# One SBUF input per blend operation, and a convolution in two passes, in a deformable-convolution kernel

## The chip, the cores and the metric

The kernel runs on one core of a Trainium2 chip. The metric is the time on the device of one execution, in microseconds (us). The engines are named as in the profile: PE (TensorE: matmul and transpose), DVE (VectorE), ACT (ScalarE), POOL (GpSimd) and SP (SyncE), each with its own queue of instructions, held in order by semaphores. SBUF is the on-chip memory, PSUM the eight banks (2 KB per partition each) in which PE leaves its results.

## What is computed

An image `x` of 2 x 128 channels x 64 x 64 goes through a layer norm over channels, then through a block of four deformable convolutions with 1, 1, 9 and 49 taps (60 in all) and 256 outputs each, then group norms, a 1 x 1 fuse and a spectral (FFT) stage. The change lies in the deformable convolutions alone. For each of the 60 taps and each pixel the reference takes four neighbouring pixels ("corners") at a position that is itself computed by convolutions, weighs them, adds them and multiplies the sum with the tap's weights:

```python
offset = conv2d(x, off_w, off_b, pad)
mask = 2.0 * jax.nn.sigmoid(conv2d(x, mod_w, mod_b, pad))
...
v00, v01 = gather(y0, x0), gather(y0, x0 + 1)
v10, v11 = gather(y0 + 1, x0), gather(y0 + 1, x0 + 1)
sampled = (v00 * (1 - wy) * (1 - wx) + v01 * (1 - wy) * wx + v10 * wy * (1 - wx) + v11 * wy * wx) * mask
y = einsum('bckhw,ock->bohw', sampled, reg_w)
```

All of it is in float32.

## The kernel before

`stage_branches` does this work. Its 2 x 4096 pixels are cut into 16 groups (`NG`) of 512 pixels, and the 60 taps of a group follow one another, so there are 960 steps `n` (`NT`), step n being tap `k` of group `g`. Each engine has a loop over n, written out by hand. For a step:

- POOL issues four indirect DMAs (`gather`, L472), one for each 128 pixels. Each takes 128 row numbers from the SBUF tile `om` and brings 128 rows of 2 KB, a row holding the four corners of a pixel, 128 channels each. They land in `G[k % 6]`, one of six buffers (`RING`); POOL waits until the step six before has been blended (`blended`, L486).
- ACT scales the first corner in place with four activations (`corner0`, L507).
- DVE (`blend`) multiplies corners 1 to 3 by their weights, read with stride 0 from the SBUF tile `omw` (L623, 1536 elements per partition); adds corners 2 and 3 to corners 0 and 1 (L629, 1024 elements); and adds the two sums into one of three `acc` buffers (L633, 512 elements). The sum is what frees `G`. Each of the three reads two inputs from SBUF.
- PE turns `acc` (four transposes into one of two PSUM banks `ps_t`, L742); ACT copies that to `sT` (`copy_out`, L515) two steps after the blend of the same tap; PE contracts `sT` with the tap's weights `R` into `ps_y` (`contract`, L754), two steps (`LAG`) behind the turn.

Beside it PE computes the offsets and masks of the next group: 49 taps of a 7 x 7 convolution with 180 output columns, 128 of them into `ps_c` (L724) and 52 into `ps_c2` (L725), spread by `share_at` over 52 of 56 steps (36 steps for the first). `copy_conv` takes the two banks to SBUF, `turn_conv` turns them into the bank `ps_o` in four tiles of 128 pixels, and DVE makes row numbers and weights of each tile (`rows` and `weights`, L585 to L613), sixteen instructions in two neighbouring steps. At tap 54 of a group DVE also takes statistics of finished outputs (`measure`, L639). The eight PSUM banks are all in use: `ps_y` two, `ps_t` two, `ps_c`, `ps_c2`, `ps_o` and `ps_side` (normalisation of the second image) one each.

## Time and profile before

| | |
|---|---|
| time, median of 3 runs | 7700.79 us (7696.2 to 7709.71) |
| the profiled execution | 7701.75 us, its span 7700.1 us |
| granted TensorE clock, mean | 0.886 of 2.4 GHz |
| first to last blend of `stage_branches` | 167 to 6229 us of the span |

The span is the time from the first to the last instruction. The profile gives, for each engine, the time in which it was busy, groups of instructions by line with the mean length of one, and what ended the idle time before them; the trace gives single instructions in order of time. A DMA's row on POOL is the time in which POOL prepares it, not the transfer.

### The profile page before, as it was taken

To read this page: it belongs to the slowest core of one execution; us is meant where nothing else is said; L and a number is where in the kernel's file an instruction comes from. 1 tells how busy PE (TensorE), PEld (TensorE's weight loads), DVE (VectorE), ACT (ScalarE), POOL (GpSimd) and SP (SyncE) were. 2 spreads that over 40 slices of the span, in tenths; PEclk is the share of its full clock that TensorE was granted. 3 is DMA by queue.
4 is the path that set the end of the run, shared out by engine and by line. 5 is a ranking of instruction groups with operands and counts; after the bars stand their busy time and mean duration, and the time that the engine had idled before them with its cause. 6 is when DMAs were issued, how large, how long until landed. Compare 5 with 4: busy or idle time off the path is not lost. (4 is left out here: it accounts for less than half of the span.)

```text
span 7700.1 us, 63816 instructions
## 1 busy us (share of the span) xinstructions
PE 5662.3 (74%) x16608; PEld 2740.6 (36%) x16608; DVE 4714.2 (61%) x5704; ACT 2581.2 (34%) x6416; POOL 5182.4 (67%) x4363
## 2 busy tenths in 40 slices
PE   4877777777777777677777777777555665899998
PEld 3322323222222222222222222222222222677777
DVE  3575766666666656666565656565656534566665
ACT  1232323322222222323232323232322243366664
POOL 2888888888888888888888888888888820122221
PEclk9989889898899898998989998989777677899999
DMA  7666666666666666666665656565656565555555
GB/s 216 171 194 175 194 180 198 183 180 175 176 177 178 175 178 173 181 171 186 168 186 162 188 163 187 164 183 163 184 164 176 163 214 193 183 150 148 147 153 175
DMA packets 593353, 1362.45 MB, mean 177 GB/s; under 512 B 108104, under 2 KB 273864, under 8 KB 591312
## 3 DMA queue, kind: packets, MB, share of 16 engines
q0 software_dynamic: 327680, 1044.66, 48.4%
q1 hardware_dynamic: 237088, 295.80, 12.1%
q10 hardware_dynamic: 28336, 19.10, 0.8%
q8 instruction: 104, 1.70, 0.1%
q14 instruction: 145, 1.19, 0.1%
HBM read 1243.49 MB, written 115.72 MB: 177 GB/s over the span
## 5 line engine op out<-in xcount | busy, mean ns | idle before, releaser
L472 POOL DMA_INDIRECT G<-table,om x3840 | 4912.7, 1279 | 1222.1 <-issue 947.4
L623 DVE SCALAR_TENSOR_TENSOR G<-G,omw 128x1536 f32<-128x1536 f32 x960 | 1687.9, 1758 | 1924.9 <-DMA G<-table,om 1898.0
L507 ACT ACTIVATE G<-G,om 128x128 f32<-128x128 f32 x3840 | 1226.8, 390 | 4131.5 <-DMA G<-table,om 4100.0
L754 PE MATMUL ps_y<-sT,R 128*128 128x512 f32 x3840 | 2312.3, 735 | 91.1 <-ACT sT L515 86.0
L742 PE MATMUL ps_t<-ident,acc 128*128 128x128 f32 x3840 | 724.9, 319 | 1675.7 <-DVE acc L633 1655.3
L742 PEld LDWEIGHTS ps_t<-ident,acc 128*128 128x128 f32 x3840 | 468.3, 157 | 2519.0 <-DVE acc L633 2415.6
L629 DVE SCALAR_TENSOR_TENSOR G<-G 128x1024 f32<-128x1024 f32 x960 | 1176.3, 1225 | 104.6 <-DVE G L623 4.1
L754 PEld LDWEIGHTS ps_y<-sT,R 128*128 128x128 f32 x3840 | 807.5, 233 | 769.7 <-issue 642.7
L1487 POOL DMA_DIRECT2D ut<-spec_dram x512 | 262.7, 513 | 892.0 <-PE ps_v L1568 636.8
L1553 DVE TENSOR_TENSOR vl<-ps_v,vh 128x512 fp32r<-128x512 f32 x1024 | 658.4, 686 | 333.1 <-ACT vh L1502 333.1
L724 PE MATMUL ps_c<-xr,wom 128*128 128x512 f32 x1470 | 805.9, 631 | 0.0
L725 PE MATMUL ps_c<-xr,wom 128*52 128x512 f32 x1470 | 787.4, 616 | 0.0
L633 DVE SCALAR_TENSOR_TENSOR acc<-G 128x512 f32<-128x512 f32 x960 | 664.4, 692 | 103.9 <-DVE G L629 4.6
L1502 ACT ACTIVATE vh<-ps_v 128x512 fp32r<-128x512 f32 x1024 | 579.6, 596 | 298.0 <-PE ps_v L1568 273.7
L515 ACT ACTIVATE sT<-ps_t 128x512 f32<-128x512 f32 x960 | 552.3, 575 | 61.7 <-PE ps_y L754 55.9
L724 PEld LDWEIGHTS ps_c<-xr,wom 128*128 128x128 f32 x1470 | 311.0, 215 | 414.4 <-issue 414.4
L1591 PE MATMUL ps_yf<-vh,mh 128*128 128x512 f32 x1024 | 413.8, 404 | 0.0
L1591 PE MATMUL ps_yf<-vh,ml 128*128 128x512 f32 x1024 | 411.4, 402 | 0.0
L1591 PE MATMUL ps_yf<-vl,mh 128*128 128x512 f32 x1024 | 409.4, 400 | 0.0
L1568 PE MATMUL ps_v<-tt,ut 96*128 96x512 f32 x1024 | 368.1, 401 | 15.4 <-DMA tt<-kern_dram 10.0
L725 PEld LDWEIGHTS ps_c<-xr,wom 128*52 128x52 f32 x1470 | 125.9, 125 | 595.8 <-issue 595.8
L1568 PEld LDWEIGHTS ps_v<-tt,ut 96*128 96x128 f32 x1024 | 194.7, 191 | 71.2 <-DMA ut<-spec_dram 19.2
(181 smaller groups left out, 2183.8 us busy)
## 6 DMA issues: line engine op xcount, KB each, us to landing
tt<-kern_dram SPq DMA_DIRECT2D x512, 192.0 KB, 3.4
G<-table,om POOLq DMA_INDIRECT x3840
y_dram<-yb SPq DMA_DIRECT2D x64, 512.0 KB
yin<-y_dram SPq DMA_DIRECT2D x16, 2048.0 KB, 8.4
ut<-spec_dram POOLq DMA_DIRECT2D x256, 96.0 KB, 3.3
spec_dram<-spec_hi SPq DMA_DIRECT2D x64, 256.0 KB, 2.6
ut<-spec_dram POOLq DMA_DIRECT2D x256, 48.0 KB, 3.0
om_dram<-om_next SPq DMA_DIRECT2D x60, 150.0 KB
```

The lines of the kernel that those rows point to most:

```text
L472: pool.indirect_dma_start(G[k % RING][:, j, :], None, tables[g // GI], bass.IndirectOffsetOnAxis(ap=om[g % 2][:, j, 0, k:k + 1].bitcast(I3 ...
L507: last = nc.scalar.activation(G[k % RING][:, j, 0:C], G[k % RING][:, j, 0:C], ACT.Copy, scale=om[g % 2][:, j, 1, k:k + 1])
L623: nc.vector.scalar_tensor_tensor(part(1, 4), part(1, 4), 1.0, omw[g % 2][:, :, k:k + 1].to_broadcast([128, 12, C]) .rearrange("p (j c) d - ...
L629: nc.vector.scalar_tensor_tensor(part(0, 2), part(2, 4), 1.0, part(0, 2), ALU.mult, ALU.add)\
L633: nc.vector.scalar_tensor_tensor(acc[n % 3][:, :, :], whole(1), 1.0, whole(0), ALU.mult, ALU.add)\
L724: nc.tensor.matmul(ps_c[:, :], cols[:, 0:128], rows, start=(tap == 0), stop=(tap == 48))
L725: last = nc.tensor.matmul(ps_c2[:, :], cols[:, 128:128 + REST], rows, start=(tap == 0), stop=(tap == 48))
L742: last = nc.tensor.transpose(ps_t[n % 2][:, 128 * j:128 * j + 128], acc[n % 3][:, j, :], ident[:, :])
L754: last = nc.tensor.matmul(ps_y[:, half, :], R[:, k, 128 * half:128 * half + 128], sT[n % 2][:, :], start=(k == t0), stop=(k == ends[br] - 1))
L1502: nc.scalar.activation(vh[c][:, n, :, :], spread(ps_v[n % BANKS]), ACT.Copy).then_inc(v_high, 1)
L1553: nc.vector.tensor_tensor(vl[c][:, n, :, :], spread(ps_v[n % BANKS]), vh[c][:, n, :, :].bitcast(F32), ALU.subtract).then_inc(v_low, 1)
L1591: last = nc.tensor.matmul(ps_y[q][:, :], m[:, c, k, :], v[c][:, :, k, :], start=(c == 0 and k == 0 and n == 0), stop=(c == 1 and k == KF - ...
```

## The change

The blend works with at most one input in SBUF per DVE instruction. A new PSUM bank `ps_w` holds the weights of 30 taps, copied there every 30 steps by DVE (`spread`: 360 elements per partition); the multiplication reads its weights from it. A new bank `ps_a` holds the running sum: ACT writes the scaled first corner there in place of into `G`, and three DVE additions of 512 elements each follow, the first two in place in `ps_a`, the last from `ps_a` into `acc`. So three DVE instructions become four, by `tensor_tensor` in place of `scalar_tensor_tensor`. As there is one `ps_a`, `corner0(n)` waits for the blend of step n-1.

The two banks are made free thus: `ps_t` becomes one bank (a turn waits for the copy of the turn before, and ACT copies one step earlier than before), and `ps_c2` shares a bank with `ps_o`. For that the convolution goes through its 49 taps twice, first the 128 columns, then the 52; before the first of the 52 PE waits until `ps_o` has been read by DVE (`om_read`).

The diff, without the hunks that only rename a slice or a constant:

```diff
@@ -259,10 +260,13 @@
         xt1 = xw[:, :].rearrange("p (j c) -> p j c", j=4)
 
         ps_y = ctx.enter_context(nc.psum_tensor("ps_y", [128, 2, CH], F32))
-        ps_t = [ctx.enter_context(nc.psum_tensor(f"ps_t{h}", [C, CH], F32)) for h in range(2)]
+        ps_t = ctx.enter_context(nc.psum_tensor("ps_t", [C, CH], F32))
+        ps_a = ctx.enter_context(nc.psum_tensor("ps_a", [128, 4, C], F32))
+        ps_w = ctx.enter_context(nc.psum_tensor("ps_w", [128, 4 * 3, HALF_TAPS], F32))
         ps_c = ctx.enter_context(nc.psum_tensor("ps_c", [128, CH], F32))
-        ps_c2 = ctx.enter_context(nc.psum_tensor("ps_c2", [REST, CH], F32))
-        ps_o = ctx.enter_context(nc.psum_tensor("ps_o", [128, 3 * TAPS], F32))
+        ps_shared = ctx.enter_context(nc.psum_tensor("ps_shared", [128, CH], F32))
+        ps_c2 = ps_shared[0:REST, :]
+        ps_o = ps_shared[:, 0:3 * TAPS]
         ps_s = ctx.enter_context(nc.psum_tensor("ps_side", [128, 4, C], F32))
 
         params = sem("om_params")
...
@@ -285,7 +289,8 @@
         gathered = [sem(f"gathered{s}") for s in range(RING)]
         first_corner = sem("first_corner")
         weighted = sem("weighted")
-        paired = sem("paired")
+        weights_spread = sem("weights_spread")
+        added = sem("corners_added")
         blended = sem("blended")
         turned = sem("turned")
         copied = sem("copied")
...
@@ -332,7 +338,7 @@
             for gr in range(1, NG):
                 i = n - BEGIN[gr]
                 if 0 <= i < SPAN[gr]:
-                    return gr, 49 * i // SPAN[gr], 49 * (i + 1) // SPAN[gr]
+                    return gr, 98 * i // SPAN[gr], 98 * (i + 1) // SPAN[gr]
             return None
 
         def group_at(n, late):
...
@@ -503,8 +509,9 @@
             def corner0(n):
                 g, k = divmod(n, TAPS)
                 act.wait_ge(gathered[k % RING], (n // RING) * 64 + 64)
+                act.wait_ge(blended, n + RING)
                 for j in range(4):
-                    last = nc.scalar.activation(G[k % RING][:, j, 0:C], G[k % RING][:, j, 0:C], ACT.Copy,
+                    last = nc.scalar.activation(ps_a[:, j, :], G[k % RING][:, j, 0:C], ACT.Copy,
                                                 scale=om[g % 2][:, j, 1, k:k + 1])
                 last.then_inc(first_corner, 1)
 
...
@@ -512,7 +519,7 @@
                 act.wait_ge(turned, n + 4)
                 if n >= 2:
                     act.wait_ge(summed, n - 1)
-                nc.scalar.activation(sT[n % 2][:, :], ps_t[n % 2][:, :], ACT.Copy).then_inc(copied, 1)
+                nc.scalar.activation(sT[n % 2][:, :], ps_t[:, :], ACT.Copy).then_inc(copied, 1)
 
             def evacuate(g, br):
                 act.wait_ge(summed, g * TAPS + ends[br])
...
@@ -552,8 +559,8 @@
                     evacuate(g, ends.index(k - LAG))
                 if k == LAG and g:
                     evacuate(g - 1, NBR - 1)
-                if LAG <= n < NT + LAG:
-                    copy_out(n - LAG)
+                if 1 <= n <= NT:
+                    copy_out(n - 1)
                 m = tile_at(n, 5, 2)
                 if m is not None:
                     sigmoid(m)
...
@@ -615,23 +622,33 @@
                 assert st.n == WEIGHT_STEPS
                 dve.sem_inc(offsets_ready, 1)
 
+            def spread(n):
+                g, k = divmod(n, TAPS)
+                if g:
+                    dve.wait_ge(om_loaded[g % 2], 32 * ((g + 1) // 2))
+                else:
+                    dve.wait_ge(offsets_ready, 4)
+                nc.vector.tensor_copy(ps_w[:, :, :], omw[g % 2][:, :, k:k + HALF_TAPS]).then_inc(weights_spread, 1)
+
             def blend(n):
                 g, k = divmod(n, TAPS)
-                part = lambda lo, hi: G[k % RING][:, :, lo * C:hi * C].rearrange("p j (c d) -> p j c d", c=hi - lo)
-                whole = lambda c: G[k % RING][:, :, c * C:(c + 1) * C]
+                corner = lambda c: G[k % RING][:, :, c * C:(c + 1) * C]
+                three = G[k % RING][:, :, C:4 * C].rearrange("p j (c d) -> p j c d", c=3)
+                h = k % HALF_TAPS
                 dve.wait_ge(gathered[k % RING], (n // RING) * 64 + 64)
-                nc.vector.scalar_tensor_tensor(part(1, 4), part(1, 4), 1.0,
-                                               omw[g % 2][:, :, k:k + 1].to_broadcast([128, 12, C])
-                                               .rearrange("p (j c) d -> p j c d", j=4),
-                                               ALU.mult, ALU.mult).then_inc(weighted, 1)
+                dve.wait_ge(weights_spread, n // HALF_TAPS + 1)
+                nc.vector.tensor_tensor(three, three, ps_w[:, :, h:h + 1].to_broadcast([128, 12, C])
+                                        .rearrange("p (j c) d -> p j c d", j=4), ALU.mult).then_inc(weighted, 1)
                 dve.wait_ge(first_corner, n + 1)
                 dve.wait_ge(weighted, n + 1)
-                nc.vector.scalar_tensor_tensor(part(0, 2), part(2, 4), 1.0, part(0, 2), ALU.mult, ALU.add)\
-                    .then_inc(paired, 1)
+                nc.vector.tensor_tensor(ps_a[:, :, :], corner(1), ps_a[:, :, :], ALU.add).then_inc(added, 1)
+                if h == HALF_TAPS - 1 and n + 1 < NT:
+                    spread(n + 1)
+                dve.wait_ge(added, 2 * n + 1)
+                nc.vector.tensor_tensor(ps_a[:, :, :], corner(2), ps_a[:, :, :], ALU.add).then_inc(added, 1)
                 dve.wait_ge(turned, n + 1)
-                dve.wait_ge(paired, n + 1)
-                nc.vector.scalar_tensor_tensor(acc[n % 3][:, :, :], whole(1), 1.0, whole(0), ALU.mult, ALU.add)\
-                    .then_inc(blended, 1)
+                dve.wait_ge(added, 2 * n + 2)
+                nc.vector.tensor_tensor(acc[n % 3][:, :, :], corner(3), ps_a[:, :, :], ALU.add).then_inc(blended, 1)
 
             def measure(g, br):
                 dve.wait_ge(evacuated, g * NBR + br + 3)
...
@@ -666,6 +683,7 @@
             for m in range(AHEAD):
                 rows(m)
                 weights(m)
+            spread(0)
             for n in range(NT + 5):
                 g, k = divmod(n, TAPS)
                 if n < NT:
...
@@ -717,13 +735,16 @@
                     pe.wait_ge(xr_loaded[gr % 2], 16 * ((gr + 1) // 2))
                     if gr > 1:
                         pe.wait_ge(cT_copied, gr - 1)
-                for tap in range(lo, hi):
+                if lo <= 49 < hi:
+                    pe.wait_ge(om_read, 4 * gr + 1)
+                for i in range(lo, hi):
+                    rest, tap = divmod(i, 49)
                     ky, kx = divmod(tap, 7)
                     rows = xr[gr % 2][:, ky:ky + 8, kx:kx + W]
                     cols = wom[:, tap, :, :].rearrange("c a t -> c (a t)")
-                    nc.tensor.matmul(ps_c[:, :], cols[:, 0:128], rows, start=(tap == 0), stop=(tap == 48))
-                    last = nc.tensor.matmul(ps_c2[:, :], cols[:, 128:128 + REST], rows, start=(tap == 0), stop=(tap == 48))
-                if hi == 49:
+                    last = nc.tensor.matmul(ps_c2 if rest else ps_c[:, :], cols[:, 128:128 + REST] if rest else cols[:, 0:128],
+                                            rows, start=(tap == 0), stop=(tap == 48))
+                if hi == 98:
                     last.then_inc(convolved, 1)
 
             def turn_conv(m):
...
@@ -736,10 +757,10 @@
 
             def turn(n):
                 pe.wait_ge(blended, n + 1 + RING)
-                if n >= 2:
-                    pe.wait_ge(copied, n - 1)
+                if n >= 1:
+                    pe.wait_ge(copied, n)
                 for j in range(4):
-                    last = nc.tensor.transpose(ps_t[n % 2][:, 128 * j:128 * j + 128], acc[n % 3][:, j, :], ident[:, :])
+                    last = nc.tensor.transpose(ps_t[:, 128 * j:128 * j + 128], acc[n % 3][:, j, :], ident[:, :])
                 last.then_inc(turned, 1)
 
             def contract(n):
```

In the order of instructions this is as follows. On DVE, at the first steps of the stage (`G0` and `G1` are gather buffers, `omw0` the weights in SBUF), before:

```order
L623 SCALAR_TENSOR_TENSOR G0<-G0,omw0 128x4x384 [waits om_step,gathered0]
L629 SCALAR_TENSOR_TENSOR G0<-G0 128x4x256 [waits weighted,first_corner]
L633 SCALAR_TENSOR_TENSOR acc0<-G0 128x512 [waits paired,turned]
L623 SCALAR_TENSOR_TENSOR G1<-G1,omw0 128x4x384 [waits gathered1]
L629 SCALAR_TENSOR_TENSOR G1<-G1 128x4x256 [waits weighted,first_corner]
```

and after:

```order
L631 COPY ps_w<-omw0 128x360 [waits om_step,offsets_ready]
L640 TENSOR_TENSOR G0<-G0,ps_w 128x4x384 [waits weights_spread,gathered0]
L644 TENSOR_TENSOR ps_a<-G0,ps_a 128x512 [waits weighted,first_corner]
L648 TENSOR_TENSOR ps_a<-G0,ps_a 128x512 [waits corners_added]
L651 TENSOR_TENSOR acc0<-G0,ps_a 128x512 [waits corners_added,turned]
L640 TENSOR_TENSOR G1<-G1,ps_w 128x4x384 [waits weights_spread,gathered1]
```

Three rows of a step became four, with `ps_w` and `ps_a` as the second input. On ACT, at the same steps (`om0` holds the first corner's weights), before:

```order
L507 ACTIVATE G0<-G0,om0 128x128 [waits gathered0]
L507 ACTIVATE G0<-G0,om0 128x128 x3
L507 ACTIVATE G1<-G1,om0 128x128 [waits gathered1]
L507 ACTIVATE G1<-G1,om0 128x128 x3
L507 ACTIVATE G2<-G2,om0 128x128 [waits gathered2]
```

and after:

```order
L514 ACTIVATE ps_a<-G0,om0 128x128 [waits blended,gathered0]
L514 ACTIVATE ps_a<-G0,om0 128x128 x3
L514 ACTIVATE ps_a<-G1,om0 128x128 [waits blended,gathered1]
L514 ACTIVATE ps_a<-G1,om0 128x128 x3
L522 ACTIVATE sT0<-ps_t 128x512 [waits turned]
```

The scaled corner now goes to `ps_a` and waits for the blend before, and the first copy of a turned tap (`sT0`) stands ahead of the third step's corner, where it stood behind it. On PE, in a group's convolution, before:

```order
L742 MATMUL ps_t0<-ident,acc2 128x128 x4
L754 MATMUL ps_y<-sT0,R 128x512 x2
L724 MATMUL ps_c<-xr0,wom 128x512
L725 MATMUL ps_c2<-xr0,wom 52x512
L742 MATMUL ps_t1<-ident,acc0 128x128 x4
```

and after, in the second pass:

```order
L763 MATMUL ps_t<-ident,acc1 128x128 x4
L775 MATMUL ps_y<-sT0,R 128x512 x2
L745 MATMUL ps_shared<-xr0,wom 52x512 x2
L763 MATMUL ps_t<-ident,acc2 128x128 x4
L775 MATMUL ps_y<-sT1,R 128x512 x2
```

A step has two matmuls of the convolution as before (a single one in six of the 52 steps), but both of the same columns.

## Rows read from the trace of the kernel before

**Rows 1.** The page, busy time of each engine over the span.
```profile
PE 5662.3 (74%) x16608; PEld 2740.6 (36%) x16608; DVE 4714.2 (61%) x5704; ACT 2581.2 (34%) x6416; POOL 5182.4 (67%) x4363
```

**Rows 2.** Stage, first to last blend: length; PE, PEld, DVE, ACT, POOL; clock, DMA.
```profile
167.00:6229.00 6062.00, 4307.34 (x10788) 1707.66 (x10788) 3841.88 (x4078) 1796.19 (x5041) 4890.23 (x3817) 0.87 0.62 177
```

**Rows 3.** The page's groups: busy us, mean ns | idle before, releaser.
```profile
L472 POOL DMA_INDIRECT G<-table,om x3840 | 4912.7, 1279 | 1222.1 <-issue 947.4
L623 DVE SCALAR_TENSOR_TENSOR G<-G,omw 128x1536 f32<-128x1536 f32 x960 | 1687.9, 1758 | 1924.9 <-DMA G<-table,om 1898.0
...
L629 DVE SCALAR_TENSOR_TENSOR G<-G 128x1024 f32<-128x1024 f32 x960 | 1176.3, 1225 | 104.6 <-DVE G L623 4.1
...
L633 DVE SCALAR_TENSOR_TENSOR acc<-G 128x512 f32<-128x512 f32 x960 | 664.4, 692 | 103.9 <-DVE G L629 4.6
```

**Rows 4.** Timeline, one step: start us, length us, instruction [idle before].
```profile
2006.47 0.95 POOL L472 DMA_INDIRECT G<-table,om  x1 [0.30 <-issue]
2006.80 1.28 ACT L507 ACTIVATE G<-G,om 128x128 f32<-128x128 f32 x4 [3.07 <-DMA G<-table,om]
2006.80 1.76 DVE L623 SCALAR_TENSOR_TENSOR G<-G,omw 128x1536 f32<-128x1536 f32 x1 [1.91 <-DMA G<-table,om]
...
2007.72 1.66 POOL L472 DMA_INDIRECT G<-table,om  x1 [0.30 <-issue]
2007.98 0.57 ACT L515 ACTIVATE sT<-ps_t 128x512 f32<-128x512 f32 x1
...
2008.66 1.23 DVE L629 SCALAR_TENSOR_TENSOR G<-G 128x1024 f32<-128x1024 f32 x1
...
2009.68 1.02 POOL L472 DMA_INDIRECT G<-table,om  x1 [0.30 <-issue]
...
2009.99 0.69 DVE L633 SCALAR_TENSOR_TENSOR acc<-G 128x512 f32<-128x512 f32 x1
```

**Rows 5.** Timeline, just behind it: DVE's statistics and a gather.
```profile
2010.60 3.65 DVE L639 BATCH_NORM_STATS2 ystats<-yb 128x6 f32<-128x512 f32 x6
...
2012.26 0.95 POOL L472 DMA_INDIRECT G<-table,om  x1 [0.30 <-issue]
```

**Rows 6.** Timeline: a DVE addition of PSUM and SBUF, and a gather.
```profile
5069.73 0.35 DVE L585 TENSOR_TENSOR P<-ps_o,base 128x180 f32<-128x180 f32 x1 [1.41 <-PE ps_o L734]
5069.89 0.95 POOL L472 DMA_INDIRECT G<-table,om  x1 [0.30 <-issue]
```

**Rows 7.** L472 in the stage: ns min/median/max, first and last start.
```profile
L472 POOL DMA_INDIRECT G<-table,om x3817: 942/1017/2526, 166.5 to 6221.9; - x191
```

**Rows 8.** Waits in the stage: us in total, times, longest us.
```profile
POOL G L472 <- DVE acc L633: 224.3, 726, 3.4
```

**Rows 9.** Groups of DVE by shape: busy us, mean ns | idle before.
```profile
L1553 DVE TENSOR_TENSOR vl<-ps_v,vh 128x512 fp32r<-128x512 f32 x1024 | 658.4, 686 | 333.1 <-ACT vh L1502 333.1
...
L594 DVE TENSOR_TENSOR gt<-fl,P 128x120 f32<-128x120 f32 x64 | 18.2, 284 | 2.2
...
L1046 DVE TENSOR_TENSOR accum<-t_rb,t_xg 128x512 f32 x16 | 17.5, 1100 | 20.4 <-DMA t_xg<-in_x 20.3
```

**Rows 10.** Timeline of PE: a step with convolution, at full clock.
```profile
2034.51 0.66 PE L742 MATMUL ps_t<-ident,acc 128*128 128x128 f32 x4 [2.02 <-DVE acc L633]
2035.00 1.88 PE L754 MATMUL ps_y<-sT,R 128*128 128x512 f32 x4
2036.72 1.02 PE L724 MATMUL ps_c<-xr,wom 128*128 128x512 f32 x2
2037.67 1.06 PE L725 MATMUL ps_c<-xr,wom 128*52 128x512 f32 x2
```

**Rows 11.** Timeline: the last gather and the start of the last blend.
```profile
6221.87 1.02 POOL L472 DMA_INDIRECT G<-table,om  x1 [0.30 <-issue]
...
6225.32 1.76 DVE L623 SCALAR_TENSOR_TENSOR G<-G,omw 128x1536 f32<-128x1536 f32 x1 [2.45 <-DMA G<-table,om]
```

**Rows 12.** Twenty us with a store beside the gathers; columns as in rows 2.
```profile
2370.00:2390.00 20.00, 12.97 (x37) 5.08 (x36) 11.43 (x10) 8.49 (x23) 15.73 (x15) 0.91 0.83 264
```

More of the change, by code:

```diff
@@ L20 @@
 WIN_TAP = 35
+HALF_TAPS = 30
 NG = B * GI
@@ L315, in stage_branches @@
         LAG = 2
+        assert TAPS == 2 * HALF_TAPS
         X_FIRST, X_STEP = 14, 28
@@ L530, in copy_conv @@
                 nc.scalar.activation(cT[:, :], ps_c[:, :], ACT.Copy)
-                nc.scalar.activation(cT2[:, :], ps_c2[:, :], ACT.Copy).then_inc(cT_copied, 1)
+                nc.scalar.activation(cT2[:, :], ps_c2, ACT.Copy).then_inc(cT_copied, 1)
             def root_x(c):
@@ L584, in rows @@
                 dve.wait_ge(om_done, m + 1)
-                st.then(nc.vector.tensor_tensor(P[:], ps_o[:, :].rearrange("p (a t) -> p a t", a=3), base[:], ALU.add))
+                st.then(nc.vector.tensor_tensor(P[:], ps_o.rearrange("p (a t) -> p a t", a=3), base[:], ALU.add))
                 dve.sem_inc(om_read, 1)
@@ L705, in convolve_first @@
                 pe.wait_ge(om_read, m + 1)
-                out = ps_o[:, :].rearrange("p (a t) -> p a t", a=3)
+                out = ps_o.rearrange("p (a t) -> p a t", a=3)
                 for tap in conv_taps:
```

## The prediction, made before the changed kernel ran

> **What bounds the kernel now.** No engine looks full over the whole span: PE is busy 74% of it, POOL 67%, DVE 61% [rows 1]. So the first view to read is the stage that the change touches. It takes 6062 us of the 7700, and in it POOL is busy 4890 us and DVE 3842 [rows 2]. POOL's 81% understates it: between two gathers there are 0.30 us in which POOL waits for nothing that is shown [rows 4]. The 3840 gathers take 4912.7 us [rows 3] and the gaps 3840 x 0.305 = 1171, together 6084 us, the whole of the stage and the little before it. A step of four gathers lasts 4 x (1.279 + 0.305) = 6.34 us. DVE meanwhile waits 1898 us for gathered data [rows 3], 2 us in each of 960 steps. POOL's own waits for a blend come to 224 us over 726 times, which is the 0.3 us that it spends between gathers anyway, the longest 3.4 us [rows 8]. So POOL alone sets the pace, and DVE, ACT and PE follow.
>
> **Why is a gather 1.279 us?** The shortest is 0.942 us, the longest 2.526, the median 1.017 [rows 7]. One step shows why. The gather at 2006.47 took 0.95 us: it began before the multiplication. The next began at 2007.72, while the multiplication of 2006.80 ran to 8.56, and ended at 9.38, that is 0.82 us behind it. The third began at 2009.68 within L629 (8.66 to 9.89) and ended at 10.70, again 0.81 behind [rows 4]. A gather, which reads its row numbers from SBUF, that starts under a DVE instruction with two SBUF inputs makes no progress until that one ends. One that starts under the statistics (one SBUF input, 2010.60 to 2014.25) takes 0.95 [rows 5]. And one that started at 5069.89 under an addition of PSUM and SBUF, which ended at 5070.08, took 0.95 [rows 6]; held as the others were it would have ended at 5070.90, after 1.01. That last row is the only kind of the new instructions that the trace shows under a gather, and it is thin, 0.06 us apart.
>
> **The change, part by part.**
>
> *Gathers.* With no two-input instruction in the blend they go back to 0.945 us: 3840 x (1.279 - 0.945) = 1283 us less on the engine that sets the end. Two-input instructions remain in `rows` and `weights`. They last 0.284 us at most [rows 9] and hold a gather only if it starts in their first 0.16 us (0.284 less the 0.945 - 0.82 that a gather can spare), at most 0.16 us then. Some ten in each of 60 tiles is 600 instructions of 0.28 us, 3% of the stage, so some 120 gathers, 5 us; I take 5 to 20. POOL's stage becomes 3840 x (0.945 + 0.305) = 4800 us, 5.00 us a step.
>
> *DVE.* The question is whether DVE can do a step in 5.00 us. `tensor_tensor` of 512 elements with one PSUM and one SBUF input takes 686 ns [rows 9], where the two-SBUF L633 takes 692 [rows 3]. The multiplication keeps its 1536 elements, so 1758 ns. Gaps between dependent instructions of a step are 0.10 (8.56 to 8.66, 9.89 to 9.99) [rows 4]. So 1.76 + 3 x 0.69 + 3 x 0.105 + 0.05 to start = 4.19 us. Other work of DVE in the stage is 3842 - 1688 - 1176 - 664 = 314 us [rows 2, 3], 0.33 a step; the 32 `spread` copies of 360 elements are at most 32 x 1.1 = 35 us by the slowest 512-element row [rows 9], 0.02 to 0.04 a step. Sum 4.55 us, against 5.00: DVE stays below, with 9% to spare. What no row shows is DVE writing to PSUM, in place at that. Its bounds: below, the 0.69 of the rows with a PSUM input (less is possible only in the fixed part, 0.15 of 0.69); above, the slowest addition of 512 elements in the trace, 1.10 us [rows 9]. I take 0.69, since the row with a PSUM input is within 1% of the one without.
>
> The Trainium skill ("Perfetto Trace Analysis", Optimizing Scalar/DVE Operations) speaks against the change here: about 60 ns of access for a DVE instruction on SBUF, about 125 on PSUM. By that four instructions would cost 0.26 us more, 4.8 a step, nearly POOL's 5.0; the row of 686 ns shows no such difference.
>
> *ACT.* Its four activations take 1.28 us [rows 4]. They now start only when the blend before has ended, but so does the multiplication (1.76 us) beside which they run, so the first addition still waits for the multiplication, with 0.4 us in hand: no cost. If PSUM as target made them slower, the cover is those 0.4 us; behind that a step grows by the excess, with 0.45 us of DVE's slack still to use. ACT's step is 1.28 + 0.57 of 5.00. Queued behind the new wait for `blended` are the copies `sT` and the evacuations. They have time: the copy of step n-1 can start 1.3 us after its blend, and the turn of step n comes 5 us after it.
>
> *PE.* At full clock a step with convolution lasts from 2034.51 to 2038.73, 4.22 us [rows 10], against 5.00. The single `ps_t` asks that the copy of n-1 be done before the turn of n; that copy waits for a contraction that ends 2.37 us into the step (2036.88) and for ACT's 1.28, so it is done by about 3.0 us, inside the convolution or inside PE's idle time. The two passes of the convolution are the same 1470 matmuls in number. The wait for `om_read` is for tiles read some twenty steps before: nothing. In the first group 26 of 36 steps get three such matmuls, 5.2 us, and the other ten 4.2, mean 4.9: even with POOL. Of the clock: PE's mean in the stage is 0.87 with 4307 us of work, 4.49 a step [rows 2]; rows at full clock are followed by 2.02 us of waiting for the blend [rows 10]. A shorter step takes idle time out, so I expect the mean clock to rise and not fall, and take nothing for it.
>
> *The ring.* When the last gather ends (6222.89) its blend starts 2.43 us later [rows 11] and takes 3.9, while POOL needs the freed buffer five steps on: 5 x 6.34 + 0.3 - 6.3 = 25.7 us of slack before, 5 x 5.00 + 0.3 - 2.4 - 4.2 = 18.7 after. DVE's side work comes in bunches (a tile in two steps, four tiles in eight, some 15 us), in which it falls behind by 15 - 8 x 0.8 = 9 us: covered.
>
> *DMA.* The share of the DMA engines would go from 0.62 to 0.62 x 6062/4790 = 0.78 and the rate from 177 to 224 GB/s. Twenty us with a store beside gathers show 264 GB/s at 0.83 [rows 12]. So no bound, though with less air.
>
> **Sum.** Against the profiled span of 7700: -1283 for the gathers, +10 for the small holds, +1 for a longer last blend (4.19 for 3.9), +20 for moments in which bunches use up the ring (a guess of 1 to 2 us a group): 6448. The profiled execution's 7701.75 lies 1 us above both its span and the median of 7700.79, so nothing is added: **6450 us**.
>
> **Rivals.**
>
> *Bunches break through.* DVE's 9 us, a burst of late landings and a PE step at half clock (its 4.22 us of work longer) fall together. Against it are the 18.7 us; for it, that everything now runs at 85 to 91% of POOL's pace and recovers only 0.45 us a step. Ten us a group, 16 groups, is 160: 6600. The same holds if ACT, waiting for a late PE in its copy, delays the next corner.
>
> *Additions in place are slow.* Two of three at 1.10 us: DVE 4.55 + 0.82 = 5.37 us a step, 960 x 5.37 = 5155, +355 over POOL: about 6790.
>
> *Transfers become the bound*, if random reads don't reach 224 GB/s steadily. At 200 the stage is 6062 x 177/200 = 5365: 7000.
>
> *The hold stays.* If any running DVE instruction held a gather, four shorter ones would hold as much as three: about 7700, no change. Rows 5 and 6 speak against it. The Trainium skill ("SBUF — State Buffer", Who interferes with whom) infers that a `tensor_tensor` does not stall the preparation of a DMA, as it takes only the shared read interface; by that there would be no hold to remove. The row of 1.66 us shows one.
>
> *Slower than before.* PSUM access at the slow row's 1.10 us per 512 elements in all four instructions, 3.1 us for the multiplication with its stride-0 operand and 3 x 1.10: 6.4 + 0.37 + 0.37 = 7.1 us a step, 960 x 7.1 = 6820, against 6062 now: 8460. It decides from 6.3 us a step on, that is 1.75 us more for the four than I take. Against it is the 686 ns row.
>
> **Chances.** Forecast (6415 to 6520) 0.66; bunches (to 6700) 0.14; slow additions 0.07; transfers 0.05; hold stays 0.03; slower 0.05. The range takes in the first three, 6405 to 6800. 0.2% of the time is about what can be told from no change. Faster is all but the last two, 0.92; same 0.03; slower 0.05.
>
> **What would show it.** L478 (the gather) at a median near 0.95 us with hardly any above 1.1; POOL's gaps still 0.30, and its waits for blends still 0.3 us each; DVE's additions near 0.69 and the multiplication 1.76; steps of 5.0 us; DVE still waiting for gathers, 0.5 us a step in place of 2; DMA share near 0.78. The forecast is wrong if POOL waits for `blended` for long, if an addition into `ps_a` takes over 0.85 us, or if landings come late while POOL runs freely.

## The result, and the profile after

The changed kernel takes 7722.8 us (median of 20 runs, 7706 to 7763), the kernel before 7702.1 us in the same jobs: ratio 1.003, 95% interval 1.002 to 1.0041. The forecast was 6450 us and faster; the time is the same to 0.3%, on the slow side. The profiled execution's span is 7722.6 us.

The stage's row (busy time by engine, then granted clock, DMA share, GB/s) and the page's costliest groups:

```profile
167.00:6229.00 6062.00, 4126.85 (x10748) 1739.09 (x10748) 3918.51 (x5046) 1789.93 (x5013) 3607.78 (x3816) 0.84 0.61 177
```
```profile
L478 POOL DMA_INDIRECT G<-table,om x3840 | 3630.7, 945 | 2503.5 <-DVE acc L651 1231.1
...
L763 PE MATMUL ps_t<-ident,acc 128*128 128x128 f32 x3840 | 722.4, 319 | 1878.5 <-ACT sT L522 1254.3
L644 DVE TENSOR_TENSOR ps_a<-G,ps_a 128x512 f32<-128x512 f32 x960 | 668.4, 696 | 1825.7 <-ACT ps_a L514 1124.1
L522 ACT ACTIVATE sT<-ps_t 128x512 f32<-128x512 f32 x960 | 573.3, 597 | 3596.8 <-remote 1939.1
L640 DVE TENSOR_TENSOR G<-G,ps_w 128x1536 f32<-128x1536 f32 x960 | 1678.3, 1748 | 21.3 <-DVE om_next L620 12.2
...
L514 ACT ACTIVATE ps_a<-G,om 128x128 f32<-128x128 f32 x3840 | 1186.9, 359 | 514.2 <-DVE acc L651 356.1
```

Against [rows 2, 3]: POOL's busy time in the stage fell from 4890 to 3608 us, a gather from 1279 to 945 ns, as forecast (4912.7 - 3630.7 = 1282, forecast 1283). All of it came back as waiting. POOL's idle time ahead of gathers grew to 2503.5 us, of which 1231 is waiting for DVE's blend; before, that wait was 224 us, in pieces of some 0.3 us [rows 8]. DVE no longer waits for gathered data (21 us ahead of L640). It waits for ACT's first corner (L514), ACT stands at its copy `sT` (L522), and the releaser printed there is "remote": no end of an instruction on this core explains the start. The waits, who for whom, with us in total, times and the longest:

```profile
ACT sT L522 <- remote: 1939.1, 235, 15.3
PE ps_t L763 <- ACT sT L522: 1254.3, 254, 13.2
POOL G L478 <- DVE acc L651: 1231.1, 278, 10.8
...
DVE ps_a L644 <- ACT ps_a L514: 1124.1, 289, 12.7
```

Read downwards, it is one chain: the copy waits for something unnamed, then PE for the copy, DVE for ACT (the next corner is queued behind the copy), POOL for DVE. In the kernel before, the copy has one such "remote" wait, of 1.5 us, and all of ACT one more. One case in order of time, PE, ACT, DVE and POOL of the changed kernel:

```profile
2010.20 0.60 PE L763 MATMUL ps_t<-ident,acc 128*128 128x128 f32 x4
2010.63 1.88 PE L775 MATMUL ps_y<-sT,R 128*128 128x512 f32 x4
2012.35 1.90 PE L745 MATMUL ps_c<-xr,wom 128*128 128x512 f32 x4
2019.02 1.09 PE L763 MATMUL ps_t<-ident,acc 128*128 128x128 f32 x4 [4.77 <-issue]
```
```profile
2009.70 1.24 ACT L514 ACTIVATE ps_a<-G,om 128x128 f32<-128x128 f32 x4 [0.39 <-issue]
2018.28 0.60 ACT L522 ACTIVATE sT<-ps_t 128x512 f32<-128x512 f32 x1 [7.33 <-remote]
```
```profile
2013.51 1.75 DVE L640 TENSOR_TENSOR G<-G,ps_w 128x1536 f32<-128x1536 f32 x1
2020.03 0.70 DVE L644 TENSOR_TENSOR ps_a<-G,ps_a 128x512 f32<-128x512 f32 x1 [4.77 <-issue]
```
```profile
2013.85 0.94 POOL L478 DMA_INDIRECT G<-table,om  x1 [0.30 <-issue]
2015.10 0.95 POOL L478 DMA_INDIRECT G<-table,om  x1 [0.30 <-issue]
```

The copy at 2018.28 needs the transposes that end at 2010.80 and the contraction that ends at 2012.51. It starts 5.8 us after the later one. The trace's record of semaphore updates shows what it waited for: the increment of the transposes stands at 2013.30, that of the contraction at 2018.19. Up to the end of the stage 266 of 695 recorded increments of the transposes come over 0.5 us after the modelled end (half of these over 4.3 us, the longest 13.3); in the kernel before, 2 of 883. Of DVE's and ACT's recorded increments none is late in either, but the record has gaps: of the changed kernel's 961 increments by the last addition it holds 482. No wait of any engine for DVE or ACT, though, shows as "remote" in the changed kernel; all of them are waits for PE. POOL meanwhile gathers on, one every 1.25 us. So 44% of the steps take 4.0 to 4.6 us, faster than forecast, 32% take over 6, and the mean is 6.34, just what it took before (6.32); by chance, as far as the runs tell, since other gathers give other means (below).

The kernel before has the same thing once, and with the old blend, which has no operand in PSUM. Its densest stretch of gathers is that from 1492 to 1525 us: 24 distances between gathers, 1.37 us on average, where the next densest such stretch has 1.43 and the mean of the stage is 1.58. There, from 1521 to 1531 us, stand the only recorded increments of PE in the whole stage that come over 1 us late (five, by 1.1 to 5.8 us), and ACT waits for "remote":

```profile
1523.21 0.60 ACT L542 ACTIVATE xnp<-ps_side 128x512 f32<-128x512 f32 x1 [7.41 <-remote]
...
1528.29 0.60 ACT L515 ACTIVATE sT<-ps_t 128x512 f32<-128x512 f32 x1 [1.53 <-remote]
```

### The profile page after: what moved, and what is told of

The parts are those of the page before. It is cut to its first block and busy times, and to the rows that moved or that the text cites. A ratio compares the mean times of both kernels' runs of the same rounds, so it can differ in the third digit from the quotient of the medians.

```text
span 7722.6 us, 66678 instructions
## 1 busy us (share of the span) xinstructions
PE 5495.9 (71%) x16608; PEld 2779.5 (36%) x16608; DVE 4812.2 (62%) x6696; ACT 2585.9 (33%) x6416; POOL 3900.4 (51%) x4363
## 3 DMA queue, kind: packets, MB, share of 16 engines
q14 instruction: 167, 1.37, 0.1%
## 5 line engine op out<-in xcount | busy, mean ns | idle before, releaser
L478 POOL DMA_INDIRECT G<-table,om x3840 | 3630.7, 945 | 2503.5 <-DVE acc L651 1231.1
L775 PE MATMUL ps_y<-sT,R 128*128 128x512 f32 x3840 | 2237.4, 714 | 78.0 <-issue 45.2
L644 DVE TENSOR_TENSOR ps_a<-G,ps_a 128x512 f32<-128x512 f32 x960 | 668.4, 696 | 1825.7 <-ACT ps_a L514 1124.1
L522 ACT ACTIVATE sT<-ps_t 128x512 f32<-128x512 f32 x960 | 573.3, 597 | 3596.8 <-remote 1939.1
L640 DVE TENSOR_TENSOR G<-G,ps_w 128x1536 f32<-128x1536 f32 x960 | 1678.3, 1748 | 21.3 <-DVE om_next L620 12.2
L514 ACT ACTIVATE ps_a<-G,om 128x128 f32<-128x128 f32 x3840 | 1186.9, 359 | 514.2 <-DVE acc L651 356.1
L745 PE MATMUL ps_shared<-xr,wom 128*52 128x512 f32 x1470 | 731.6, 618 | 0.0
L745 PE MATMUL ps_c<-xr,wom 128*128 128x512 f32 x1470 | 730.5, 618 | 0.0
L651 DVE TENSOR_TENSOR acc<-G,ps_a 128x512 f32<-128x512 f32 x960 | 659.9, 687 | 103.0 <-DVE ps_a L648 2.3
L648 DVE TENSOR_TENSOR ps_a<-G,ps_a 128x512 f32<-128x512 f32 x960 | 667.0, 695 | 31.8
L745 PEld LDWEIGHTS ps_shared<-xr,wom 128*52 128x52 f32 x1470 | 158.3, 129 | 553.8 <-issue 553.8
```

The source lines that it names most:

```text
L478: pool.indirect_dma_start(G[k % RING][:, j, :], None, tables[g // GI], bass.IndirectOffsetOnAxis(ap=om[g % 2][:, j, 0, k:k + 1].bitcast(I3 ...
L514: last = nc.scalar.activation(ps_a[:, j, :], G[k % RING][:, j, 0:C], ACT.Copy, scale=om[g % 2][:, j, 1, k:k + 1])
L640: nc.vector.tensor_tensor(three, three, ps_w[:, :, h:h + 1].to_broadcast([128, 12, C]) .rearrange("p (j c) d -> p j c d", j=4), ALU.mult). ...
L644: nc.vector.tensor_tensor(ps_a[:, :, :], corner(1), ps_a[:, :, :], ALU.add).then_inc(added, 1)
L648: nc.vector.tensor_tensor(ps_a[:, :, :], corner(2), ps_a[:, :, :], ALU.add).then_inc(added, 1)
L651: nc.vector.tensor_tensor(acc[n % 3][:, :, :], corner(3), ps_a[:, :, :], ALU.add).then_inc(blended, 1)
```

## The experiments

Distance means the time from the start of one gather to the start of the next; hold means the wait of the copy for "remote", in total. A step is the mean from the first weighting to the last, over 959 steps. The expectations count copies that start late, which gives other numbers than the hold. Where no interval stands beside a time, it is a single run.

**Is it the handshake?** The first four runs asked whether the new layout of PSUM causes it (theory H: the single `ps_t`; W: the order of PE's two waits) or the new accesses to PSUM or the faster gathers (P).

The layout, the two-pass convolution and the earlier copy on the kernel before, with its old blend:

```diff
-        ps_t = [ctx.enter_context(nc.psum_tensor(f"ps_t{h}", [C, CH], F32)) for h in range(2)]
+        ps_t = ctx.enter_context(nc.psum_tensor("ps_t", [C, CH], F32))
...
-                if LAG <= n < NT + LAG:
-                    copy_out(n - LAG)
+                if 1 <= n <= NT:
+                    copy_out(n - 1)
```


> The kernel before, with the changed PSUM layout alone: one ps_t bank (a turn waits for the copy of the turn before, the copy stands one step earlier), ps_c2 and ps_o in one bank, the convolution in two passes. The blend is the old one. In the changed kernel ACT's copy sT starts up to 14 us behind the end of all that it waits for, 264 times of 920, 1532 us in sum, and DVE, POOL and PE stand behind it. Theory H (the handshake over one ps_t brings these stalls): they appear here too, on top of a step of 6.34 us or hidden in the 2 us that DVE waits; 7700 to 8600 us, ACT's copy late by over 0.5 us in well over 100 steps. Theory P (the accesses of DVE and ACT to PSUM, or the faster gathers, bring them): none of them here, copy late in under 10 steps, 7700 us.

7693.9 us, ratio 0.9989 (0.9979 to 0.9999), hold 10.8 us in 2 waits. The layout costs nothing.

The changed kernel with two `ps_t` again, beside one with a single `ps_t`, both with the second image's normalisation left out to free the bank (the first image's table serves for both, so the output is not the reference's; this "side work" is left out in all kernels below that don't say whole):

```diff
-                if n >= 1:
-                    pe.wait_ge(copied, n)
+                if n >= 2:
+                    pe.wait_ge(copied, n - 1)
```


> The changed kernel with two ps_t banks as before, the copy two steps behind again. The bank comes from leaving out the normalisation of the second image (turns, statistics, table writes; image 0's table and convolution input are used twice), so part of the computation is left out: compare with the run that leaves out the same and has one ps_t. Theory H: stalls gone or hidden, a step of 5.0 to 5.3 us, 6450 to 6750 us. Theory P: they stay, 7300 to 7700 us.

> The changed kernel, one ps_t, without the normalisation of the second image (the control for the run with two). It leaves out that part of the computation. Both theories: the stalls stay, 7600 to 7720 us, since the side work is some 4 us in each of 8 steps of DVE and 32 small transposes.

7736.1 us (1.0016 to 1.0054 of before) and 7707.8 us (0.9996 to 1.0023); holds 2027 and 2054 us. Twice the buffers gain nothing, and the side work is not part of it.

PE's two waits ahead of a turn, swapped in the whole kernel:

```diff
-                pe.wait_ge(blended, n + 1 + RING)
                 if n >= 1:
                     pe.wait_ge(copied, n)
+                pe.wait_ge(blended, n + 1 + RING)
```


> The changed kernel with the two waits ahead of a turn on PE written in the other order, so that the wait for the copy is carried by the weight load and the wait for the blend stands as an instruction of its own. Theory W (PE hands on its finished increments late while it stands at a wait of its own for ACT's copy): the stalls vanish, 6450 to 6700 us. Theories H and P: no change, 7720 us.

7734.8 us, 1.0047 (1.0033 to 1.0061), hold 1969 us. H and W have fallen.

**Is it the gathers?** From here on theory Q is that the gathers disturb PE's signals, P that the chain of DVE, ACT and PE is slow by itself. Half of the gathers (`for j in range(2)` after the first ring), and none:

> The changed kernel without the second image's table (as in the run with one target bank), and after the first ring only two of a step's four gathers are issued (half of POOL's work, half of the rows moved; the blend works on stale rows in the other half, so the result is not the reference's). Theory Q (the gathers, now 0.945 us each, and the rows they move disturb something on PE's side, so that PE's signals to ACT come late): the late signals nearly vanish (under 50 of 920 copies start over 0.5 us late, against 262) and the step falls from 6.33 to what DVE allows, 4.6 to 5.0 us: 7708 - 950 x 1.3 to 1.7 us = 6100 to 6450 us. Theory P (something in DVE's, ACT's and PE's own chain gives 6.33 us a step, whatever the gathers do): step 6.2 to 6.4, time 7600 to 7730 us, the copies late as before.

> As the run with half of the gathers, but none at all is issued after the first six steps: DVE, ACT and PE work on stale rows. Theory Q: no late copies, step 4.5 to 4.7 us (DVE's 4.55 us sets it), 6100 to 6250 us. Theory P: step 6.2 to 6.4 us, copies late, 7600 to 7730 us. A step between the two (5.0 to 6.0) with late copies would say that both have a part.

5930.7 and 5924.0 us, steps of 4.47 and 4.46 us, and no "remote" wait at all, below both expected times. The chain of DVE, ACT and PE, with all its accesses to PSUM, runs at the price that the prediction had worked out (4.55). With half of the gathers POOL waits for DVE nearly every step:

```profile
POOL G L475 <- DVE acc L646: 2165.5, 954, 9.4
```

**PE's work?** All but 4 of 98 convolution matmuls of a group left out:

```diff
                     rest, tap = divmod(i, 49)
+                    if 0 < tap < 48:
+                        continue
```


> The changed kernel without the second image's table, and 94 of the 98 convolution matmuls of each group are left out (only the first and the last tap of each bank are kept), so the offsets are not the reference's and the rows gathered are others. PE has about a third less to do and fewer instructions. Theory F (PE's own instruction stream: its signals are late about every 128 of its instructions): stalls stand further apart in steps (7 or more in place of 4.7) and the step falls towards 5.3 to 5.8 us, 7000 to 7300 us. Theory Q or P: the step stays at 6.1 to 6.4 us, 7500 to 7700 us, since the few stretches without a convolution showed 6.15 us before.

7566.9 us, hold 1976 us, step 6.18: as Q and P had it, and not PE's instruction stream.

**Their succession?** A small memset and a wait for it ahead of each gather:

```diff
+                    pool.memset(spare[:], 0.0).then_inc(paced, 1)
+                    pool.wait_ge(paced, 4 * (n - RING) + j + 1)
                     gather(g, k, j)
```


> The changed kernel without the second image's table, with a small memset on POOL and a wait for its end ahead of each gather after the first ring: gathers of 0.945 us that start some 1.45 us apart, so POOL allows a step of 5.6 to 6.0 us. Theory Q, if what disturbs PE is the close succession of the gathers: the late copies fall to under 100 and the step is POOL's own, 5.6 to 6.0 us, 7050 to 7400 us. Theory P, or a total that each step owes: 6.3 us or more, 7700 us or more, copies late as often.

7384.1 us at a distance of 1.39 us: POOL has more to do and the kernel is 320 us faster than its like without a pause (7707.8). But the late copies, which should have nearly vanished, did not: the hold stays at 1977 us in 319 waits, and the step is 5.98, above POOL's 5.56. The step isn't a fixed debt either: it fell with the rate.

**Bytes, or POOL's work?** Rows of 1 KB in place of 2 KB; and the same bytes loaded by SP's queue, with no gather:

```diff
-                pool.indirect_dma_start(G[k % RING][:, j, :], None, tables[0],
+                    dst, rows = G[k % RING][:, j, 0:2 * C], tables[0].rearrange("r (h c) -> (r h) c", h=2)
+                pool.indirect_dma_start(dst, None, rows,
```


> The changed kernel without the second image's table; after the first ring each of the four gathers still makes 128 rows' worth of descriptors, but of 1 KB rows in place of 2 KB (other rows than the reference's; half of the blend's input is stale). Theory D (the bytes that the gathers move into SBUF delay PE's signals): the late copies nearly vanish (under 50 of 920), POOL's 5.0 us set the step, 6350 to 6550 us. Theory G (POOL's making of descriptors in close succession does it, whatever they move): copies late as in the run with one target bank (over 200), step 6.2 to 6.4, 7600 to 7750 us.

```diff
+                    for j in range(4):
+                        sp.dma_start(G[(n + RING) % RING][:, j, :], tables[0][128 * j + n:128 * j + n + 128, :])\
+                            .then_inc(loaded[n % RING], 16)
```


> The changed kernel without the second image's table; after the first ring POOL gathers nothing, and SP's queue loads the same number of bytes in rows of the same length (four plain loads of 128 consecutive table rows a step, behind the same wait; not the reference's rows). Theory G: no late copies, step 4.5 to 4.9 us, 5950 to 6300 us. Theory D: copies late (over 150), step over 5.5 us, over 6900 us.

Half of the bytes: 7749.3 us. All of the bytes without POOL: 6059.8 us. Rows of the waits of the first, then from 2000 to 4500 us of the second (columns as above):

```profile
ACT sT L521 <- remote: 2055.2, 237, 15.2
```
```profile
2000.00:4500.00 2500.00, 2075.83 (x5997) 869.36 (x5996) 2224.41 (x2799) 1044.24 (x2865) 0.00 (x0) 0.95 0.75 244
```

244 GB/s at a DMA share of 0.75 disturb nobody (the changed kernel moves 176 there). The loads are of consecutive rows, so this clears the bytes and the landings in SBUF, not random reads; the run with half rows has as many of those as before, and only the run with 64 rows, below, halves them. Theory G stands so far: what holds PE's signals is POOL gathering too fast.

**Distance, rate, lead, or rows?** The same pause, once a step:

```diff
                 pool.wait_ge(blended, n + 1)
+                pool.memset(spare[:], 0.0).then_inc(paced, 1)
+                pool.wait_ge(paced, n - RING + 1)
                 for j in range(4):
```


> The changed kernel without the second image's table, with one memset of 448 elements on POOL ahead of a step's four gathers in place of a small one ahead of each: the same 5.6 us a step on POOL as in the paced run, but the four gathers start 1.25 us apart. If the succession of single gathers counts: 7600 us or more, as unpaced. If the mean rate over a step counts: 7300 to 7450 us, as paced.

7436.6 us, hold 1883 us, at a mean distance of 1.36 us: near the evenly paced 7384, far from 7708. The rate over a step counts, not the nearest neighbour.

Three gathers a step (`for j in range(3)`):

> The changed kernel without the second image's table; after the first ring three of a step's four gathers are issued (a quarter of the blend works on stale rows). They stand 1.25 us apart, 3.75 us a step on POOL, which then waits for DVE (4.5 us a step): on average one gather in 1.5 us. If the rate over a step or more counts (limit near 1.4 to 1.47 us a gather): no or few late copies, step 4.5 to 4.6 us, 5930 to 6050 us. If the distance of neighbours counts: copies late (over 100) and the step 5.0 us or more, 6400 us or more.

6304.2 us, step 4.86, hold 621 us in 136 waits: neither expectation. The mean distance is 1.62 us, but in steps without other DVE work (4.0 us) three gathers make 1.33 each. That fits a limit that acts over several gathers and is crossed in such stretches; it doesn't prove it.

The whole kernel, with POOL at most three steps ahead:

```diff
-                pool.wait_ge(blended, n + 1)
+                pool.wait_ge(blended, n + 4)
```


> The whole changed kernel, unpaced, but POOL waits for the blend three steps later than it has to, so it is at most three steps ahead of DVE in place of six. If the rate counts and a hold ends once POOL stops: holds as often but shorter, since POOL runs dry sooner; step 5.5 to 6.1 us, 6950 to 7500 us. If the lead is the cause: no late copies, POOL's 5.0 us a step, 6450 to 6600 us. If neither matters: 7690 to 7740 us.

7724.5 us, 1.0033 (1.0019 to 1.0048), hold 2079 us. The lead is nothing, and holds don't get shorter when POOL runs dry sooner, as the first of the three expectations had it.

Gathers of 64 rows in place of 128:

```diff
-                pool.indirect_dma_start(G[k % RING][:, j, :], None, tables[0],
+                p = 128 if g == 0 and k < RING else 64
+                pool.indirect_dma_start(G[k % RING][0:p, j, :], None, tables[0],
```


> The changed kernel without the second image's table; after the first ring each of the four gathers takes 64 rows in place of 128 (half of the blend works on stale rows). If the limit is one of rows or descriptors (128 in some 1.42 us, so 64 in 0.71 us): POOL needs over 0.5 us for 64 rows and 0.3 us between two, so it stays under the limit, no late copies, 5930 to 6100 us. If it is one of gathers (one in 1.42 us), four in DVE's 4.5 us are too many: copies late (over 150), step 5.6 us or more, 7000 us or more.

```profile
L476 POOL DMA_INDIRECT G<-table,om x3840 | 3468.4, 903 | 2838.3 <-DVE acc L647 1479.7
```
```profile
ACT sT L518 <- remote: 2073.1, 220, 15.2
```

7894.0 us, slower than with 128. A gather of half the rows takes 903 ns, so they follow each other at 1.21 us in place of 1.25, and the step grows to 6.52. With half of the rows, bytes and random reads, the holds are all there: it is a limit on gathers.

**Where is the limit?** Three whole kernels, memsets of 160, 112 and 88 elements:

> The whole changed kernel with a memset of 160 elements and a wait for its end ahead of each gather after the first ring: gathers some 1.47 us apart, POOL's floor 5.9 us a step. If the late signals vanish at this distance, POOL sets 5.9 us: 7300 to 7380 us. If they stay as in the paced run (1398 us in sum, step 5.98 at a floor of 5.56 us): 7380 to 7500 us. If pacing only moved the wait, 7650 or more.

> The whole changed kernel with a memset of 112 elements and a wait ahead of each gather: gathers 1.43 us apart, POOL's floor 5.72 us a step. If the limit lies under 1.43 us, no late copies and 7318 - 960 x 0.16 = 7165 us (7140 to 7200). If it lies between 1.43 and 1.47 us, late copies come back: 7300 to 7400 us.

> The whole changed kernel with a memset of 88 elements and a wait ahead of each gather: gathers 1.41 us apart, POOL's floor 5.64 us. If the limit lies under 1.41 us: 7165 - 960 x 0.08 = 7090 us. If it lies between 1.41 and 1.43 us, late copies cost more than the floor gives: 7200 to 7350 us.

| distance, us | POOL's floor a step | step measured | hold, us | time, us | ratio to before (95%) |
|---|---|---|---|---|---|
| 1.25, changed kernel | 5.00 | 6.34 | 1939 | 7722.8 | 1.003 (1.002-1.0041) |
| 1.39, no side work | 5.56 | 5.98 | 1977 | 7384.1 | one run |
| 1.41 | 5.64 | 6.01 | 2083 | 7395.1 | 0.9593 (0.9575-0.9611) |
| 1.43 | 5.72 | 5.76 | 1054 | 7164.9 | 0.9304 (0.9289-0.932) |
| 1.47 | 5.88 | 5.92 | 0 | 7318.6 | 0.9497 (0.9482-0.9513) |

At 1.47 us no hold is left and POOL sets the pace: the memset, the gather, and DVE waiting for data, as in the kernel before:

```profile
3000.44 0.95 POOL L480 DMA_INDIRECT G<-table,om  x1 [0.27 <-POOL spare L496]
3001.39 0.25 POOL L496 MEMSET spare<- 128x160 f32 x1
3001.91 0.95 POOL L480 DMA_INDIRECT G<-table,om  x1 [0.27 <-POOL spare L496]
```
```profile
3000.93 1.75 DVE L644 TENSOR_TENSOR G<-G,ps_w 128x1536 f32<-128x1536 f32 x1 [1.69 <-DMA G<-table,om]
```

At 1.43 holds come back (333 of 735 recorded increments of the transposes come over 0.5 us late, the longest 8.5) but they are short, and POOL hardly stops for them, 11.5 us in all. So the time came out as expected for no late copies, 7165 us, though the condition, no late copies, did not hold. The longest waits on ACT:

```profile
ACT ps_a L518 <- DMA G<-table,om: 1372.4, 438, 10.6
...
ACT sT L526 <- remote: 1053.7, 250, 8.0
```

At 1.41 the holds are doubled and reach POOL, which waits 279 us for the blend; 0.02 us a gather cost 230 us, more than the worst that was expected (7350 us). The best version is the changed kernel paced at 1.43 us: **7164.9 us, 7% under the kernel before**. It sits close to the edge; 1.47 is the one to choose where a margin is wanted.

## Why the prediction was wrong

- *Gathers* were right: 945 ns each, 1282 us less. So was the reading of [rows 4 to 6] that a DVE instruction with two SBUF inputs holds a gather and one with PSUM and SBUF inputs doesn't. The Trainium skill ("SBUF — State Buffer", Who interferes with whom) infers that a `tensor_tensor` does not stall the preparation of a DMA. This case's traces differ for two SBUF inputs: the old blend's `scalar_tensor_tensor` held gathers, and 14 gathers of the changed kernel that started under a `tensor_tensor` with both inputs in SBUF (`fr<-P,fl`, 128x120), with over 0.14 us of it left, took 1.03 us on average. Under the new blend's instructions, with one SBUF input each, the mean stayed 0.945.
- *DVE* was right: additions 696, 695 and 687 ns against 690, the weighting 1748 against 1758, no price for PSUM as a target or in place. The higher access time for PSUM that the Trainium skill gives for DVE ("Perfetto Trace Analysis", Optimizing Scalar/DVE Operations) doesn't show in these rows. ACT's corner became shorter with PSUM as target (359 ns, before 390). Without gathers the step is 4.46 us, forecast 4.55.
- *ACT, PE, the ring*: no fault in them by themselves. The single `ps_t` and the longer wait were harmless, as said (7693.9 us with the layout alone; 4.46 us a step with both and no gathers).
- *DMA*: bytes were no bound, as said; 244 GB/s went through untroubled, though in consecutive rows. No run kept up 224 GB/s with gathered rows (194 at 1.43 us, from 2000 to 4500 us).
- *The step that failed* is the one that no term carried: "POOL's stage becomes 3840 x (0.945 + 0.305)". It took it that gathers may follow each other at 1.25 us for the whole stage, since the trace shows single ones at that distance [rows 4]. The kernel before has a mean distance of 1.58 us, and never more than seven gathers in a row at 1.25; that it can be kept up was in no row, and its one stretch of 24 distances at 1.37 us shows the late signals. At a mean distance of 1.43 us or less over many gathers PE's signals come late (at 1.47 they don't), the chain behind them stalls, and at 1.25 the gain is gone: 1.34 us a step of waiting on top of POOL's 5.00. The old blend, by holding the gathers, had paced them.
- Of the rivals, *transfers* came nearest (a limit on how fast gathers may come) but named bytes and 7000 us; *the hold stays* gave the right time by a mechanism that isn't there. *Bunches break through* named the chain (ACT, waiting in its copy for a late PE, delays the next corner), but with PE late by its own work at half clock, and at 6600 us. The sign was named in the last part (POOL waiting for `blended` for long); a cause by which PE's signals come late without late work had been given no chance.
- PE's clock in the stage fell from 0.87 to 0.84, where a rise was expected: PE idles in the holds and runs at half clock behind them (the transposes at 2019.02 take 1.09 us in place of 0.60). It is a consequence: paced at 1.43 us the clock from 2000 to 4500 us is 0.93.

**What stays open** is how gathers on POOL delay the increments of PE's semaphores and no other engine's. Shown is that it needs gathers by POOL, that it depends on their rate (over more than one gather), and that bytes, rows, POOL's lead, the number of PSUM buffers, PE's convolution and the order of the waits don't matter. That it also comes without the new accesses to PSUM rests on the one stretch of the kernel before. Whether the number of gathers per time counts or the share of the time that POOL spends in them isn't separated, since a gather took 903 ns or more on average in every run, nor is POOL's work from its DMA queue, which went away together. Whether PE's matmuls end late or only their signals can't be told, since their ends are modelled.

## What to carry to other kernels

A stall removed from an engine raises the rate of what it issues; look whether the trace of before shows that rate kept up over several periods, not only between two neighbours, and what happens in its densest stretch; if it shows neither, that is an unknown with a bound of its own. When an engine gets its time back and the kernel doesn't move, read the waits for one whose releaser is not on the core, and follow the chain from it. Where a kernel's indirect gathers follow each other for long at a mean distance below some 1.45 us (an estimate, between the 1.43 with holds and the 1.47 without, from this kernel alone), try a small pause ahead of each: slower on POOL was faster in all.

## What the runs showed that was not expected

- An engine's semaphore increments can come up to 14 us after the modelled end of the work (at 1.43 us up to 9), for PE alone, when POOL gathers at a mean distance of 1.43 us or less; at 1.47 us none did. In the profile it is a wait for "remote" on the engine that waits for PE.
- A gather of 64 rows takes 903 ns, one of 128 rows 945 to 955, of 128 rows of 1 KB 948: its time is nearly all fixed.
- Additions in place in PSUM, and with PSUM as an input, take the time of those in SBUF (695 and 687 ns against 692 [rows 3]).
- Gathers that come faster than the limit give a longer step than gathers at it: 1.21 us (64 rows) gives 6.52 us a step, 1.25 us 6.34, 1.39 us 5.98, 1.43 us 5.76.
